# Routing the second expert stage earlier: its first four groups inside the attention's last two turns, its second part beside the first tiles

## The chip, the cores and the metric

One core of a Trainium2 chip runs one program. Its engines work side by side, each through its own instruction list, in order: TensorE (PE, matrix products and transposes into the eight PSUM banks; PEld is its weight load), VectorE (DVE), ScalarE (ACT), GpSimd (POOL) and SyncE (SP, which here only starts DMAs). An engine stops at a wait until a semaphore has reached a value, and all that stands behind the wait in its list stops with it. The metric is the device time of one execution, in microseconds (us).

## The reference, cut to what matters

The program is a stack of six residual blocks on x, which is 4 x 1024 tokens of 128 channels. The change touches the end of the second and the start of the third:

```python
x = x + 0.5 * _L0_ffn_ref(_layernorm(x), router_w, w_gate, w_up, w_down)       # n = 0, experts
x = x + _L0_attn_ref(_layernorm(x), w_qkv, b_qkv, w_proj, b_proj)              # n = 1, attention
x = x + 0.5 * _L0_ffn_ref(_layernorm(x), router_w, w_gate, w_up, w_down)       # n = 2, experts again
x = x + 0.5 * _L1_ffn_ref(_layernorm(x), ...)                                  # n = 3, fp4 products
x = x + _L1_attn_ref(_layernorm(x), ...)                                       # n = 4, retention
x = x + 0.5 * _L1_ffn_ref(_layernorm(x), ...)                                  # n = 5, fp4 products

# the expert block: 8 experts of width 256, each token goes to two of them
logits = x @ router_w.T
weights, selected = sparsemixer_eval(logits, 0.01)     # two largest scores, with masked softmax weights
for e in range(8):
    h = silu(x @ w_gate[e].T) * (x @ w_up[e].T)
    out = out + dense_w[:, e:e + 1] * (h @ w_down[e].T)
```

The attention has 16 heads of 8 channels over 1024 tokens, a softmax, and the product with `w_proj`.

## The kernel before, in words

**Tokens.** The 4096 tokens are 32 tiles of 128; four tiles are a group (8 groups of 512 tokens), and four groups are a part (2 parts of 2048 tokens). x stays on chip.

**An expert stage (n = 0 and n = 2).** For each group: the layer norm (`ln_stats` and `ln_scale` on VectorE, the power -0.5 in `ln_power` on GpSimd, `moe_tokens` writes the normalised tokens, on VectorE), the transposes (`moe_transposes`, TensorE), their copy to SBUF (`moe_copy`, ScalarE), the router's product (`moe_logits`, TensorE) and the copy of the scores (`moe_scores`, VectorE). For each part of four groups: `route` (23 small VectorE instructions: the two best experts of each token), `moe_counts` (2 products on TensorE that count tokens), `find_places` (14 VectorE instructions: in which slot each token lands, ending in `place`, and which expert each tile of slots has, `expert_of`), `moe_exp` (one Exp on ScalarE) and `weigh` (4 VectorE instructions). Then `moe_scatter` writes the part's tokens into the slots in DRAM (`slots_x`): 32 indirect DMAs of 128 tokens, issued by GpSimd one after another. Each expert's slots are filled up to whole tiles of 256, 23 tiles for each part, 46 in all.

The tile loop is written out. At step i TensorE does `turned(i + 2)` (2 transposes, after the tile's slots have been loaded), `gate_up(i + 1)` (8 products, after its weights have been loaded) and `down(i)` (8 products); ScalarE copies, applies Silu and copies the result; VectorE multiplies (`hidden(i + 1)`, L732); SP loads the slots of tile i + 4 and then the weights of tile i + 3 (`moe_sp`). SP waits for all 32 scatters of a part at the first slots load of that part, tile 0 and tile 23. The results go back to DRAM and are gathered by 64 more indirect DMAs and added to x. Beside the loop of stage 2, VectorE does one step of later work (`beside`: the fp4 weights of the next block) in each of i = 0 to 19 and again from i = 35.

**The attention (n = 1).** It has 16 groups of heads and a turn i = 0 to 16 that is written out in 16 steps n; a turn runs the row maxima of group i beside the products of group i - 1. In a step TensorE makes four transposed score tiles (L1082; three banks in a ring, so it waits for ScalarE's Exp, L1171), and 4 products with the values (`values`, L1094, 8 records). Turn 16 has no maxima. Into it, at fixed steps, the kernel before puts the output projection of groups 0 to 5 (`att_project`, L1059), the transposes and the router's products of groups 0 to 3, and on VectorE `att_add` and the layer norms. `route` of the first part stands at the end of turn 16.

**Around the change.** The sums of the last heads leave by SP (8 small DMAs into OC and SC), VectorE inverts them (`att_reciprocals`, two halves of 512 columns, L1210) and GpSimd multiplies them into OC (`normalised`, L1315). The projection of group 7 needs the second half of that. After it come groups 6 and 7 (projection, add, layer norm), then the transposes and scores of groups 4 to 7, then `route`, `moe_counts`, `find_places` and `weigh` of the second part, and only then the first tile. TensorE waits for both parts' places before `turned(0)`. GpSimd's order is: `ln_power` 0 to 5, the two `normalised`, 8 scatters, `ln_power` 6 and 7, 24 scatters, and 32 scatters of part 1.

Of the kernel before, what the change touches and what calls it, by code (L numbers as in the profile page):

```python
# [82 lines left out]
def macaron(nc, a, out):  # L83
    ctx = ExitStack()
    with ctx:
# [253 lines left out]
        COUNTS = {0: 5, 2: 3}  # L339
# [50 lines left out]

        def part_tiles(part):

            return slice(part * PART_TOKEN_TILES, (part + 1) * PART_TOKEN_TILES)
# [6 lines left out]
        def moe_counts(pe, n, part):  # L400
            s = moe
            pe.wait_ge(s["members"], parts_before(n) + part + 1)
            of = members[:, :, :].rearrange("p e t -> p (e t)")
            pe.matmul(bank(COUNTS[n])[:, 2 * P:3 * P], before_in_tile, of, start=True, stop=True)
            pe.matmul(bank(COUNTS[n])[:, 3 * P:4 * P], all_ones, of, start=True, stop=True).then_inc(s["counts"], 1)

        def route(dve, chain, n, part):
# [13 lines left out]
            chain.mark(dve.tensor_reduce(m[0], S, AX.X, ALU.max))  # L421
            chain(dve.tensor_scalar(A.bitcast(I32), S.bitcast(I32), 0x7FFFFFFF, None, ALU.bitwise_and))
            chain.mark(dve.tensor_tensor(F, A, b(m[0]), ALU.max))
            chain.mark(dve.tensor_tensor(X[0], S, b(m[0]), ALU.subtract))
            chain.mark(dve.tensor_tensor(O1, S, b(m[0]), ALU.is_equal))
            chain(dve.tensor_tensor(D, b(m[0]), S, ALU.subtract))
            chain.mark(dve.scalar_tensor_tensor(K[0], F, JITTER, D, ALU.mult, ALU.is_ge))
            chain(dve.tensor_tensor(O1, O1, R, ALU.mult))
            chain(dve.tensor_reduce(tops, O1, AX.X, ALU.max))
            chain(dve.tensor_tensor(O1, R, b(tops), ALU.is_equal))  # L430
            chain(dve.tensor_scalar(M, O1, -1.0, 1.0, ALU.mult, ALU.add))
            chain(dve.tensor_tensor(M, M, S, ALU.mult))
            chain(dve.scalar_tensor_tensor(M, O1, MASKED, M, ALU.mult, ALU.add))
            chain(dve.tensor_reduce(m[1], M, AX.X, ALU.max))
            dve.tensor_tensor(X[1], M, b(m[1]), ALU.subtract).then_inc(s["shifted"], 1)
            chain.mark(dve.tensor_tensor(F, A, b(m[1]), ALU.max))
            chain.mark(dve.tensor_tensor(O2, M, b(m[1]), ALU.is_equal))
            chain(dve.tensor_tensor(D, b(m[1]), S, ALU.subtract))
            chain.mark(dve.scalar_tensor_tensor(K[1], F, JITTER, D, ALU.mult, ALU.is_ge))
            chain(dve.tensor_tensor(O2, O2, R, ALU.mult))  # L440
            chain(dve.tensor_reduce(tops, O2, AX.X, ALU.max))
            chain(dve.tensor_tensor(O2, R, b(tops), ALU.is_equal))
            dve.tensor_tensor(members[:, :, :].rearrange("p e t -> p t e"), O1, O2, ALU.add).then_inc(s["members"], 1)

        def weigh(dve, chain, n, part):
# [4 lines left out]
            chain(dve.tensor_tensor(shifted[:, :, t, :], shifted[:, :, t, :], kept[:, :, t, :], ALU.mult))  # L450
            chain(dve.tensor_reduce(mult[:, :, t], shifted[:, :, t, :], AX.X, ALU.add))
            chain(dve.reciprocal(mult[:, :, t], mult[:, :, t]))
            dve.tensor_scalar(mult[:, :, t], mult[:, :, t], 0.5, None, ALU.mult).then_inc(s["weighed"], 1)

        def find_places(dve, chain, n, part):
# [4 lines left out]
            earlier, in_tile = (bank(COUNTS[n])[:, (2 + k) * P:(3 + k) * P] for k in range(2))  # L460
            until_flat, slot_flat = (v[:, :, :].rearrange("p e t -> p (e t)") for v in (until, slot))
            chain(dve.tensor_tensor_scan(until_flat, restart, in_tile, 0.0, ALU.mult, ALU.add))
            chain.mark(dve.tensor_tensor(slot_flat, until_flat, in_tile, ALU.subtract))
            chain(dve.tensor_scalar(whole_tiles[:, :], until[:, :, PART_TOKEN_TILES - 1], 1.0 / SLOTS_TILE,
                                    (SLOTS_TILE - 1) / (2.0 * SLOTS_TILE), ALU.mult, ALU.add))
            chain.mark(dve.tensor_tensor(slot_flat, slot_flat, earlier, ALU.add))
            chain(dve.tensor_scalar(whole_tiles[:, :], whole_tiles[:, :], ROUND, ROUND, ALU.add, ALU.subtract))
            chain(dve.tensor_tensor_scan(tiles_until[:, :], all_ones[:, 0:EXPERTS], whole_tiles[:, :], 0.0, ALU.mult, ALU.add))
            chain.mark(dve.tensor_tensor(tiles_before[:, :], tiles_until[:, :], whole_tiles[:, :], ALU.subtract))
            chain(dve.tensor_tensor(passed[:, :, :], tile_number.unsqueeze(2).to_broadcast([P, PART_TILES, EXPERTS - 1]),  # L470
                                    tiles_until[:, 0:EXPERTS - 1].unsqueeze(1).to_broadcast([P, PART_TILES, EXPERTS - 1]), ALU.is_ge))
            chain(dve.tensor_reduce(expert_f[:, :], passed[:, :, :], AX.X, ALU.add))
# [93 lines left out]
        def moe_pe(pe, n):  # L566
# [52 lines left out]
            for i in range(STAGE_TILES):  # L619
# [1594 lines left out]
```

## Time and profile before

| | us |
|---|---|
| Median of 3 runs (1643.71 to 1650.12) | 1645.68 |
| The profiled execution: its own time | 1645.15 |
| Its span in the trace | 1643.3 |
| Busy: PE / DVE / ACT / POOL | 1380.4 / 1185.4 / 939.8 / 482.4 |
| Mean granted TensorE clock, as a share of full speed | 0.928 |

The page of the profile cuts the span in 40 slices of 41 us. A digit is the busy share of a slice in tenths; PEclk is the granted clock of TensorE, of which 9 stands for full speed or near it and 5 for half:

```profile
PE   2379995789999999999999988449987788997787
DVE  5412358649999999999999934534358996888995
ACT  0134441248888888888888875024454446664463
POOL 0773533410000001000000011473466745343211
PEclk9999996779999999999999998569997899998898
```

The attention is the long run of nines up to slice 23. Slices 24 to 26 (986 to 1109 us) are the end of the attention and the start of the second expert stage; the tile loop fills slices 27 to 29.

### The profile page before, as it was taken

To read this page: it belongs to the slowest core of one execution; us is meant where nothing else is said; L and a number is where in the kernel's file an instruction comes from. 1 tells how busy PE (TensorE), PEld (TensorE's weight loads), DVE (VectorE), ACT (ScalarE), POOL (GpSimd) and SP (SyncE) were. 2 spreads that over 40 slices of the span, in tenths; PEclk is the share of its full clock that TensorE was granted. 3 is DMA by queue.
4 is the path that set the end of the run, shared out by engine and by line. 5 is a ranking of instruction groups with operands and counts; after the bars stand their busy time and mean duration, and the time that the engine had idled before them with its cause. 6 is when DMAs were issued, how large, how long until landed. Compare 5 with 4: busy or idle time off the path is not lost.

```text
span 1643.3 us, 25865 instructions
## 1 busy us (share of the span) xinstructions
PE 1380.4 (84%) x9137; PEld 716.8 (44%) x9137; DVE 1185.4 (72%) x1894; ACT 939.8 (57%) x1965; POOL 482.4 (29%) x758
## 2 busy tenths in 40 slices
PE   2379995789999999999999988449987788997787
PEld 2279872331111111111111123349975565665576
DVE  5412358649999999999999934534358996888995
ACT  0134441248888888888888875024454446664463
POOL 0773533410000001000000011473466745343211
PEclk9999996779999999999999998569997899998898
DMA  7178753210000010001001000348861000000000
GB/s 246 46 210 241 225 177 102 64 60 20 26 26 25 26 41 25 25 30 35 25 25 41 10 8 4 116 131 261 257 193 31 18 1 1 2 2 2 1 26 26
DMA packets 97455, 116.22 MB, mean 71 GB/s; under 512 B 14368, under 2 KB 76512, under 8 KB 97104
## 3 DMA queue, kind: packets, MB, share of 16 engines
q1 hardware_dynamic: 64112, 85.72, 17.6%
q0 software_dynamic: 8192, 16.79, 3.3%
q10 hardware_dynamic: 25024, 12.06, 2.5%
q8 instruction: 73, 1.20, 0.3%
q14 instruction: 54, 0.44, 0.1%
HBM read 82.28 MB, written 35.26 MB: 72 GB/s over the span
## 4 chain that ended last, share of the span: by engine, by line
PE 57%; DVE 13%; ACT 6%; issue 5%; POOL 3%; SPq 0%; DMA 0%; POOLq 0%; ACTq 0%; DVEq 0%
PE PS L1094 15%; PE PS L1082 11%; PE PS L1071 6%; PE PS L585 5%; DVE neg_half L1225 4%; ACT probs L1171 3%; PE PS L597 3%; PE PS L1681 3%; PE PS L1769 2%; PE PS L1779 2%; POOL came L502 1%; POOL qk_all L1597 1%; PE PS L1712 1%; DVE x L516 1%; PE PS L890 1%
## 5 line engine op out<-in xcount | busy, mean ns | idle before, releaser
L1225 DVE TENSOR_REDUCE neg_half<-PS 128x2 f32<-128x1024 f32 x512 | 601.7, 1220 | 63.0 <-PE PS L1071 47.5
L1171 ACT ACTIVATE probs<-PS 128x512 f32<-128x512 f32 x1024 | 528.9, 604 | 118.5 <-PE PS L1082 118.3
L1082 PE MATMUL PS<-qk_all 51*128 51x512 bf16 x1024 | 279.9, 388 | 17.9 <-ACT probs L1171 12.3
L1094 PE MATMUL PS<-probs,Vg 128*32 128x512 f32 x2048 | 278.6, 617 | 0.0
L1082 PEld LDWEIGHTS PS<-qk_all 51*128 51x128 bf16 x1024 | 71.6, 93 | 338.7 <-ACT probs L1171 319.6
L732 DVE TENSOR_TENSOR shared<-shared,PS 128x512 f32<-128x512 f32 x92 | 63.2, 687 | 208.3 <-PE PS L585 185.6
L1071 PE MATMUL PS<-qk_all 48*128 48x512 bf16 x1024 | 196.3, 396 | 15.7 <-DVE neg_half L1225 13.5
L585 PE MATMUL PS<-slotsT,w_ring 128*128 128x256 f32 x736 | 180.3, 389 | 0.9 <-issue 0.9
L502 POOL DMA_INDIRECT came<-slots_y,place x128 | 128.4, 1003 | 120.0 <-DMA slots_y<-slots_out 83.0
L585 PEld LDWEIGHTS PS<-slotsT,w_ring 128*128 128x128 f32 x736 | 137.0, 196 | 16.8 <-issue 1.1
L487 POOL DMA_INDIRECT slots_x<-tokens_all,place x128 | 125.5, 980 | 41.9 <-issue 38.5
L1301 POOL CAST neg_p<-neg 128x32 bf16<-128x32 f32 x16 | 3.4, 213 | 405.0 <-DVE neg L1232 405.0
L1071 PEld LDWEIGHTS PS<-qk_all 48*128 48x128 bf16 x1024 | 49.5, 95 | 137.7 <-DVE neg_half L1225 131.1
L1681 PE MATMUL PS<-wguT,plane 128*128 128x352 f32 (+4 forms) x384 | 97.0, 415 | 4.1 <-ACT plane L1618 2.5
L597 PEld LDWEIGHTS PS<-w_ring,shared 128*128 128x128 f32 x736 | 96.8, 192 | 6.2 <-DVE shared L732 0.9
L597 PE MATMUL PS<-w_ring,shared 128*128 128x128 f32 x736 | 97.3, 275 | 0.6 <-ACT slots_out L654 0.6
L654 ACT ACTIVATE slots_out<-PS 128x256 f32<-128x256 f32 x92 | 35.3, 383 | 105.9 <-PE PS L597 103.4
L1944 DVE TENSOR_TENSOR shared<-PS,probs 128x512 f32<-128x512 f32 x128 | 79.4, 682 | 17.8 <-PE PS L1769 17.8
L1681 PEld LDWEIGHTS PS<-wguT,plane 128*128 128x128 f32 x384 | 70.3, 216 | 25.4 <-issue 8.5
L1597 POOL TENSOR_TENSOR qk_all<-qk_all 128x704 f32<-128x704 f32 x32 | 43.8, 1390 | 117.6 <-DVE qk_all L1444 93.6
L1690 PE MATMUL PS<-ident,qk_all 128*128 128x128 f32 (+1 forms) x192 | 37.7, 334 | 40.4 <-POOL qk_all L1597 30.2
L574 PE MATMUL PS<-ident,slots_in 128*128 128x128 f32 x184 | 36.7, 283 | 41.3 <-DMA slots_in<-slots_x 23.0
(222 smaller groups left out, 1824.4 us busy)
## 6 DMA issues: line engine op xcount, KB each, us to landing
w_ring<-in_w_experts SPq DMA_DIRECT2D x92, 384.0 KB
slots_in<-slots_x SPq DMA_DIRECT2D x92, 128.0 KB
slots_y<-slots_out ACTq DMA_DIRECT2D x92, 128.0 KB, 3.6
split<-qk_all SPq DMA_DIRECT2D x16, 384.0 KB, 3.3
qk_all<-split SPq DMA_DIRECT2D x64, 96.0 KB
qk_all<-split SPq DMA_DIRECT2D x64, 64.0 KB
slots_x<-tokens_all,place POOLq DMA_INDIRECT x128, 2.2
came<-slots_y,place POOLq DMA_INDIRECT x128
```

What stands on the lines that cost most here:

```text
L487: pool.indirect_dma_start(slots_x[part][:, :], bass.IndirectOffsetOnAxis(place[:, k, t:t + 1], 0), tokens_all[:, t, :], None).then_inc(moe ...
L502: pool.indirect_dma_start(came[:, g % 2, j, k, :], None, slots_y[part][:, :], bass.IndirectOffsetOnAxis(place[:, k, g * GT + j:g * GT + j ...
L585: last = pe.matmul(bank(b)[:, f * SLOTS_TILE:(f + 1) * SLOTS_TILE], w[:, u * FFN + f * P:u * FFN + (f + 1) * P], slotsT[:, k % 2, :], star ...
L597: last = pe.matmul(bank(1)[:, j * P:(j + 1) * P], h[:, k % 2, from_h:from_h + P], w[:, 2 * FFN + f * C:2 * FFN + (f + 1) * C], start=(f == ...
L732: dve.tensor_tensor(h[:, k % 2, :], sg[:, k % 2, :], bank(4 + k % 2), ALU.mult).then_inc(s["h"], 1)
L1071: last = pe.matmul(bank(b + strip), qs[at, slot, 0, pair, t * P:(t + 1) * P], qs[at, slot, 1, pair, half * GW:(half + 1) * GW], start=True ...
L1082: pe.matmul(bank(RING_AT + use % RING), qs[rows, slot, 1, pair, kt * P:(kt + 1) * P], qs[rows, slot, 0, pair, half * GW:(half + 1) * GW], ...
L1094: last = pe.matmul(bank(7)[j * 32:(j + 1) * 32, :], Vg[:, r % 2, kt, j, :], probs[:, n % 2, j, :], start=(kt == 0), stop=(kt == BT - 1))
L1171: act.activation(probs[:, n % 2, STRIPS * strip + pair, :], bank(RING_AT + use % RING), ACT.Exp, scale=ATT_SCALE).then_inc(s["exped"], 1)
L1225: dve.tensor_reduce(neg_half[m % 2][:, i % 2, :, at], bank(use_bank(i, m), 2).rearrange("p (s w) -> p s w", s=STRIPS), AX.X, ALU.max, nega ...
L1681: last = pe.matmul(bank(3 * k, 3)[:, to:to + w], xqT[:, (2 * k + j) * P:(2 * k + j + 1) * P], wguT[:, src:src + w], start=True, stop=True)
L1944: dve.tensor_tensor(pd[:, k % 2, g, :, :].rearrange("p j l -> p (j l)"), bank(g), k_decay[:, g * GW:(g + 1) * GW], ALU.mult).then_inc(s["d ...
```

## The change

**In the attention.** The fixed steps for the projections, transposes and router products are moved. They are counted from the start of turn 16, so -3 is step 13 of turn 15. The first part's `moe_counts` is put into turn 16 too. VectorE does `route` of the first part between the additions of groups 3 and 4 and `find_places` between those of groups 4 and 5. GpSimd puts 20 of the first part's 32 scatters among its last instructions of the attention.

```diff
+        TAIL_PROJECT = {-3: 0, -2: 1, -1: 2, 1: 3, 9: 4, 12: 5}
+        TAIL_TRANSPOSES = {1: 0, 2: 1, 4: 2, 5: 3}
+        TAIL_LOGITS = {2: 0, 4: 1, 5: 2, 7: 3}
+        TAIL_COUNTS = 11
...
-                    if not first:
-                        g = n // 2
-                        if n % 2 == 1 and g < TAIL_GROUPS:
...
-                            att_project(pe, g, g % 2)
-                        if n % 2 == 0 and 4 <= g < 4 + HEAD_GROUPS:
-                            moe_logits(pe, 2, g - 4)
-                        if n % 2 == 0 and 3 <= g < 3 + HEAD_GROUPS:
-                            moe_transposes(pe, 2, g - 3)
+                    tail = STEPS * (i - AG) + n
+                    if tail in TAIL_PROJECT:
...
+                        att_project(pe, g, g % 2)
+                    if tail in TAIL_LOGITS:
+                        moe_logits(pe, 2, TAIL_LOGITS[tail])
+                    if tail in TAIL_TRANSPOSES:
+                        moe_transposes(pe, 2, TAIL_TRANSPOSES[tail])
+                    if tail == TAIL_COUNTS:
+                        moe_counts(pe, 2, 0)
...
+            tail_add(0)
+            tail_add(1)
+            moe_tokens(dve, 2, 0)
+            tail_add(2)
+            moe_tokens(dve, 2, 1)
+            moe_scores(dve, 2, 0)
+            tail_add(3)
+            moe_tokens(dve, 2, 2)
+            moe_scores(dve, 2, 1)
+            moe_tokens(dve, 2, 3)
+            moe_scores(dve, 2, 2)
+            moe_scores(dve, 2, 3)
+            at_once(route(dve, chain, 2, 0))
+            tail_add(4)
+            at_once(find_places(dve, chain, 2, 0))
+            tail_add(5)
             att_reciprocals(dve, BATCH - 1, 0, GW)
+            att_reciprocals(dve, BATCH - 1, GW, SEQ)
...
-            for g in range(HEAD_GROUPS + 2):
+            for g in range(TAIL_GROUPS - 1):
                 ln_power(pool, 2, g)
+            moe_scatter(pool, 2, 0, 0, 2)
+            ln_power(pool, 2, TAIL_GROUPS - 1)
+            moe_scatter(pool, 2, 0, 2, 4)
             normalised(BATCH - 1, BATCH, 0, GW)
+            moe_scatter(pool, 2, 0, 4, 10)
             normalised(BATCH - 1, BATCH + 1, GW, SEQ)
```

**In the expert stage.** `route`, `find_places` and `weigh` become generators, which give up control after each instruction; `at_once` runs one to its end. In stage 2 the second part's three run beside the tiles: six instructions behind each `hidden(i + 1)` from i = 0. Their counting products stand behind `down(4)`, in a bank of their own (7), and their Exp stands in ScalarE's list at i = 4, between two Silus. TensorE's wait for the places is dropped for this stage. The later work beside the loop starts at i = 8 and runs to i = 22.

```diff
+        ROUTE_OPS, COUNTS_TILE, EXP_TILE = 6, 4, 4
...
-            moe_counts(pe, n, 1)
-            pe.wait_ge(s["place"], parts_before(n) + PARTS_MOE)
+            if n == 0:
+                moe_counts(pe, n, 1)
+                pe.wait_ge(s["place"], PARTS_MOE)
+            pe.wait_ge(s["xT"], groups_before(n) + GROUPS)
+            pe.wait_ge(s["logits"], groups_before(n) + GROUPS)
...
                 down(i)
+                if n == 2 and i == COUNTS_TILE:
+                    moe_counts(pe, n, 1)
...
+                if n == 2 and i == EXP_TILE:
+                    moe_exp(act, n, 1)
...
-                moe_scatter(pool, 2, 0, 0, 4)
+                moe_scatter(pool, 2, 0, 10, 14)
                 ln_power(pool, 2, GROUPS - 2)
                 ln_power(pool, 2, GROUPS - 1)
-                moe_scatter(pool, 2, 0, 4)
+                moe_scatter(pool, 2, 0, 14)
             moe_scatter(pool, n, 1)
...
+            second_part = itertools.chain(route(dve, chain, n, 1), find_places(dve, chain, n, 1), weigh(dve, chain, n, 1))
+            if n == 0:
+                at_once(second_part)
             hidden(0)
             for i in range(STAGE_TILES):
                 if i + 1 < STAGE_TILES:
                     hidden(i + 1)
+                for _ in range(ROUTE_OPS):
+                    next(second_part, None)
...
-                if n == 2 and (i < PART_TILES - 3 or at >= BESIDE_AT):
+                if n == 2 and (8 <= i < PART_TILES or at >= BESIDE_AT):
                     next(beside, None)
```

## Rows read from the trace of the kernel before

**Rows 1.** Chain of waits, 905 to 1100 us: start, duration, what

```profile
1029.55 0.61 ACT OTs L1178
...
1036.84 3.35 DVE SC L1210
...
1072.35 19.32 issue
```

**Rows 2.** Timeline of GpSimd: start, duration, instruction, idle time before and its releaser

```profile
1040.27 1.26 POOL L1315 TENSOR_TENSOR shared<-shared,SC 128x512 f32<-128x512 f32 x1 [22.19 <-DVE SC L1210]
1044.96 1.09 POOL L487 DMA_INDIRECT slots_x<-tokens_all,place  x1 [3.42 <-DVE place L480]
...
1054.92 2.03 POOL L325 TENSOR_TENSOR rstd<-aggr,minus_half 128x4 f32<-128x4 f32 x2
...
1086.36 0.95 POOL L487 DMA_INDIRECT slots_x<-tokens_all,place  x1 [0.30 <-issue]
...
1118.42 1.67 POOL L487 DMA_INDIRECT slots_x<-tokens_all,place  x1 [0.30 <-issue]
...
1128.60 0.96 POOL L487 DMA_INDIRECT slots_x<-tokens_all,place  x1 [0.30 <-issue]
```

**Rows 3.** Timeline of SP's queue at the first slots load

```profile
1088.59 3.38 SPq L540 DMA_DIRECT2D slots_in<-slots_x  x5
```

**Rows 4.** Timeline of VectorE: route and find_places of part 0

```profile
1024.29 0.29 DVE L421 TENSOR_REDUCE r_largest<-scores 128x16 f32<-128x128 f32 x1
...
1030.19 0.37 DVE L443 TENSOR_TENSOR p_members<-r_chosen 128x128 f32<-128x128 f32 x1
...
1040.11 0.36 DVE L462 TENSOR_TENSOR_SCAN p_until<-moe_const,PS 128x128 f32<-128x128 f32 x1
...
1044.48 0.18 DVE L480 CAST place<-p_place_f 128x32 uint32<-128x32 f32 x1
```

**Rows 5.** Timeline of TensorE, the attention's last steps

```profile
958.98 1.06 PE L1094 MATMUL PS<-probs,Vg 128*32 128x512 f32 x8
...
961.43 1.06 PE L1094 MATMUL PS<-probs,Vg 128*32 128x512 f32 x8
...
976.49 1.06 PE L1094 MATMUL PS<-probs,Vg 128*32 128x512 f32 x8
...
980.03 1.06 PE L1094 MATMUL PS<-probs,Vg 128*32 128x512 f32 x8
...
993.53 1.07 PE L1094 MATMUL PS<-probs,Vg 128*32 128x512 f32 x8
...
997.51 1.06 PE L1094 MATMUL PS<-probs,Vg 128*32 128x512 f32 x8
...
1016.53 1.94 PE L1094 MATMUL PS<-probs,Vg 128*32 128x512 f32 x8
...
1020.28 1.93 PE L1094 MATMUL PS<-probs,Vg 128*32 128x512 f32 x8
```

**Rows 6.** Windows of 4 us: busy time by engine, granted clock, DMA share, GB/s

```profile
968.00:972.00 4.00, 3.40 (x13) 1.30 (x14) 0.00 (x0) 2.02 (x5) 0.00 (x0) 0.58 0.23 33
```

**Rows 7.** Timeline of TensorE, the first tiles

```profile
1090.91 0.66 PE L574 MATMUL PS<-ident,slots_in 128*128 128x128 f32 x2 [17.05 <-issue]
...
1095.52 0.38 PE L574 MATMUL PS<-ident,slots_in 128*128 128x128 f32 x2
```

**Rows 8.** Timeline of VectorE, the tile loop

```profile
1097.72 0.69 DVE L732 TENSOR_TENSOR shared<-shared,PS 128x512 f32<-128x512 f32 x1 [1.26 <-PE PS L585]
...
1160.16 0.69 DVE L732 TENSOR_TENSOR shared<-shared,PS 128x512 f32<-128x512 f32 x1 [2.15 <-PE PS L585]
```

**Rows 9.** Timeline of ScalarE: Exp, table load and the stage's last result

```profile
1070.40 0.42 ACT L398 ACTIVATE r_shifted<-r_shifted 128x256 f32<-128x256 f32 x1 [6.33 <-DVE r_shifted L435]
1070.84 1.28 ACT L664 ACT_TABLE_LOAD   x1
...
1225.00 0.38 ACT L654 ACTIVATE slots_out<-PS 128x256 f32<-128x256 f32 x1 [1.31 <-PE PS L597]
```

More of the change, by code:

```diff
@@ L7 @@
 from concourse import mybir
+import itertools
 from contextlib import ExitStack
@@ L389, in moe_scores, with at_once @@
                             bank(LOGITS[n][g % 2])[:, 0:GT * EXPERTS].rearrange("p (t e) -> p t e", e=EXPERTS)).then_inc(s["logits"], 1)
+        def at_once(steps):
+            for _ in steps:
+                pass
         def part_tiles(part):
@@ L403, in moe_counts @@
             of = members[:, :, :].rearrange("p e t -> p (e t)")
-            pe.matmul(bank(COUNTS[n])[:, 2 * P:3 * P], before_in_tile, of, start=True, stop=True)
-            pe.matmul(bank(COUNTS[n])[:, 3 * P:4 * P], all_ones, of, start=True, stop=True).then_inc(s["counts"], 1)
+            pe.matmul(bank(COUNTS[n][part])[:, 2 * P:3 * P], before_in_tile, of, start=True, stop=True)
+            pe.matmul(bank(COUNTS[n][part])[:, 3 * P:4 * P], all_ones, of, start=True, stop=True).then_inc(s["counts"], 1)
         def route(dve, chain, n, part):
@@ L748, in moe_dve @@
                 dve.wait_ge(ld["small"], 48)
-            route(dve, chain, n, 0)
-            if n == 2:
-                att_reciprocals(dve, BATCH - 1, GW, SEQ)
-            find_places(dve, chain, n, 0)
-            weigh(dve, chain, n, 0)
+            if n == 0:
+                at_once(route(dve, chain, 0, 0))
+                at_once(find_places(dve, chain, 0, 0))
+            at_once(weigh(dve, chain, n, 0))
             if n == 2:
@@ L771, in moe_dve @@
             moe_scores(dve, n, GROUPS - 1)
-            route(dve, chain, n, 1)
-            find_places(dve, chain, n, 1)
-            weigh(dve, chain, n, 1)
+            second_part = itertools.chain(route(dve, chain, n, 1), find_places(dve, chain, n, 1), weigh(dve, chain, n, 1))
+            if n == 0:
+                at_once(second_part)
             hidden(0)
@@ L1188, in turn @@
                         exps(i - 1, n, 1)
-                    if i == AG and n % 2 == 1 and 3 <= n // 2 < 3 + HEAD_GROUPS:
-                        g = n // 2 - 3
+                    tail = STEPS * (i - AG) + n
+                    if tail in TAIL_TRANSPOSES:
+                        g = TAIL_TRANSPOSES[tail]
                         if g == 0:
@@ L1261, in att_dve, with tail_add @@
             dve.wait_ge(s["biased"], GROUPS)
-            for g in range(TAIL_GROUPS):
+            def tail_add(g):
                 att_add(dve, g, g % 2)
```

63 lines of the change are left out of this document (50 added, 13 removed).

## The prediction, on record before the changed kernel ran

> **What bounds the kernel now.** I read three views, in this order. The chain of waits comes first, around the end of the attention [rows 1]. The attention's last values end at 1029.5, the sums travel through SP, VectorE inverts them from 1036.8, and further on there are 19.3 us of "issue" from 1072.35: nothing that the profile names holds the chain, so it is a wait on something whose records lie on another engine. The timeline of GpSimd says what [rows 2]. Its first scatter starts at 1044.96, right behind `place` of part 0, which VectorE ends at 1044.66 [rows 4]; the last of the 32 starts at 1086.36 and ends at 1087.3. SP starts the slots load at 1088.59 [rows 3], 1.27 us later, and TensorE's first tile starts at 1090.91 [rows 7], 2.32 us after that. So the first tile is bound neither by TensorE nor by the second part's routing, but by one sum:
>
> first tile = place of part 0 + 46.25 us.
>
> In it are 32 scatters in 42.35 us less two `ln_power` (2.2 with the gaps), so 40.15 us or 1.26 each, 0.3 before and 3.6 behind. The third view is the tile loop on VectorE: a `hidden` takes 0.69 and waits 2.15 for TensorE [rows 8], so TensorE sets 2.84 us a tile and VectorE has 2.15 us free in each. From the first tile to the stage's last result, at 1225.0 [rows 9], it is 134.1 us.
>
> **Where place of part 0 comes to lie.** A bare attention step takes 2.45 us (958.98 to 961.43), one with a projection 3.54 (976.49 to 980.03), so a projection costs 1.09; one with a router product and transposes 3.98 (993.53 to 997.51), so the pair costs 1.53, of which some 0.5 for the transposes [rows 5]. Inserted work costs its full length, before and after alike, for TensorE waits for an Exp in each step and ScalarE for TensorE in turn. Steps 13, 14 and 15 of turn 15 take 3 x 3.54 from 958.98: step 0 of turn 16 starts its values at 969.6. Steps 0 to 6 are three bare ones (7.35), step 1 with projection and transposes (4.1) and three with a pair (11.9), and I add 1.0 because ScalarE now copies each transposed group right before the next step's Exps: step 7 at 994.0. The last router product ends at 996.1, the copy of the scores takes 0.2, `route` takes 6.3 (1024.29 to 1030.56) [rows 4]: members at 1002.5. The counts stand in step 11, after 3.4 + 2.45 + 3.54 + 2.45, so at 1005.9, and end at 1007.4; VectorE waits for them, not they for VectorE. `find_places` takes 4.55 (1040.11 to 1044.66): place at 1012.0 at full clock.
>
> The granted clock fell to 0.58 in 968 to 972 [rows 6], in steps like these, after bare steps; a half-clock step (1.2 GHz) takes 3.75 (1016.53 to 1020.28) instead of 2.45. I take two such steps before the counts, 2.6 us: place at 1014.6. Bounds: 1012.0, and 1035 if all from step 0 on runs at half clock (11 steps x 1.3, and 9 us of inserted work that would double). I take the low side, because the clock came back from 972 on in the same kind of steps; the ends stay in the range.
>
> **The first tile.** GpSimd now has more between the 32 scatters: `ln_power` of group 5 (1.0 and a gap) and both `normalised` (1.26 each and gaps [rows 2]), 4.2 us in all. First tile = 1014.6 + 46.25 + 4.2 = 1065.05, which is 25.9 earlier. What could be late next:
> - The second `normalised` stands behind 20 scatters and is reached at 1042.9. Its input needs the attention's end (I get 1022 to 1026), 7.3 us of SP and landing (1029.55 to 1036.84 [rows 1]) and 3.35 of `att_reciprocals`: 1033 to 1037. So GpSimd is late, not the sums, and 6 us or more of a slow attention end cost nothing.
> - TensorE's way to `turned(0)`. `ln_power` 6 and 7 stand behind 8 more scatters, at 1055.5 for group 6. Tokens (1.1), then two groups at 3.5 each with the low clock of an idle TensorE, and the last copy: 1064. That is within 1.3 us of the scatters. If it loses, the price is one to two us.
> - SP's weights for tiles 0 to 2 and the later weights go out before the scatters end; nothing is queued behind them that is due.
>
> **The loop.** It gains two count products behind `down(4)`, 0.5 us on the engine that sets the pace. VectorE's six instructions a tile are 1.2 to 2.3 us and lie in the free 2.15; `hidden` is due only one tile later. The 24th instruction waits for the counts, and `hidden(5)` stands behind it; TensorE needs its result only after the next `gate_up`, 1.7 us later, so it is covered. ScalarE's Exp at i = 4 stands between Silus. The trace has Exp, then a table load of 1.28 us, then Silu, with 0.02 us between [rows 9]: two switches and the Exp are 3.0 us, where `down(5)` has some 3 us of room behind the previous result. I take 0.2. The loop then costs 0.7 more, from 0.5 to 3.
>
> The Trainium skill (ScalarE: Activation LUTs, What ACT_TABLE_LOAD costs) states about 1.38 us of drain beside the 1.28 us load, 2.66 us for each switch. The row shows the load and no drain beside it. By the page ScalarE would be held for 5.7 us, and the loop would lose about 2.7 us more.
>
> **The second part's first tile, the wait that comes in place of the old one.** Before, part 1's scatters started at once behind part 0's and ended at 1129.6, long before tile 23. Now they wait for `place` of part 1, the 37th instruction beside the tiles, so behind `hidden(7)`. `hidden(1)` starts 6.8 us after the first tile (1097.72 against 1090.91 [rows 7, 8]), six tiles more are 17.0, its own length and the instruction 0.8, the loop's new cost 0.7: 25.3 after the first tile. The 32 scatters took 41.9 us here (1087.6 to 1129.56, a few of them stretched like that at 1118.42 [rows 2]): they end at +67.5, SP at +68.8, TensorE at +71.1. `turned(23)` is due 21 tiles after `turned(2)` (4.6 after the first tile [rows 7]), at +64.9 with the new cost. TensorE stops for 6.2 us. SP's list has the slots of tile 23 ahead of the weights of tile 22, so these are held back too, and `gate_up(22)` is next on TensorE: between 0 and 2.84 (a tile's loads keep up with one tile), I take 1.2. Sum 7.4 us; with scatters at their bare 40.1 us and no late weights it is 4.4, with a clock that falls in the gap some 10. TensorE sets the pace, so it catches nothing up.
>
> **The rest.** The steps beside the loop were 20 + 11 and are 15 + 11, with 25 of them holding work: the last now comes at i = 44 rather than 39, still before ScalarE gets to its product behind the loop. The gathers move with the tiles. Nothing from 1225 on changes its order.
>
> **The sum.** 25.9 - 0.7 - 7.4 = 17.8 us less. The profiled execution took 1645.15 (span 1643.3), so 1627.35; the median shown is 0.5 higher: **1627.9 us**.
>
> **The rivals.**
> - *A, no stop at tile 23* (8%): part 1's scatters would have to be some 7 us quicker than they were. Against it: each of the 128 needs its 1.26 us of GpSimd. Time 1620.5.
> - *B, the clock eats the attention's end* (9%): half of the steps from step 0 on run at half clock, place comes at 1023.6, 9 us later than I say, and with it every scatter and the first tile: 1636.9. For it: the dip at 968 [rows 6]. Against: the inserted work keeps TensorE busier there than the bare steps did.
> - *C, slower than before: the scatters stretch* (4%). All of part 1's scatters and 20 of part 0's now run while VectorE works in short instructions. The one at 1118.42 took 1.67 instead of 0.96 [rows 2], beside a 0.95 us instruction. If each of part 1's took 1.97 with its gap instead of their mean of 1.31, the stop at tile 23 would grow by 21 us: 1649. It decides from 1.87 us for each, where the gain is gone. Against it: most of part 1's scatters of before lay beside the fp4 steps and the sum grew by only 1.8 us. The Trainium skill (SBUF — State Buffer, Who interferes with whom) states the mechanism: VectorE's two-port copies and tensor_scalars lock GpSimd out of the port on which it writes descriptors, and the loser waits to the end of the instruction. The row shows a stretch of 0.7 us at most.
> - *D, TensorE's way to the first tile is much later, or the list does not run as I read it* (3%): 1645.
>
> The forecast holds with 76%, its own range 1622 to 1635. For 8 in 10 I go to 1621 and 1637, which takes in B and the bounds of the stop and of the table switches, but not place at 1035. A measurement of this kernel tells about 0.5%, 8.2 us, from no change. Faster by more than that (below 1637.5): the forecast, A and a part of B, 88%; within it 7%; slower 5%.
>
> **What would show it.** In the changed kernel: `place` of part 0 at 1012 to 1017, behind it 20 scatters before the attention's sums are normalised; the first tile 50.4 us behind place; a table load on each side of the Exp at the fifth tile with TensorE's pace nearly kept; one gap of 6 to 9 us on TensorE at tile 23, released by the slots load, and the next wait at the weights; 142 us from the first tile to the last result. The forecast is wrong if place comes after 1022, if the gap at tile 23 is missing or above 12 us, or if the loop's pace of 2.84 us breaks in the first eight tiles.

## The result, and the profile after

The changed kernel takes 1632.99 us (median of 5 runs, 1632.65 to 1635.42) beside 1647.02 for the one before on the same chip (5 runs, 1643.71 to 1652.0): ratio 0.9914, 95% interval 0.9892 to 0.9936, so 14.0 us less. The forecast was 1627.9, 17.8 us less. The profiled execution takes 1632.65, span 1630.8: 12.5 us less than the profiled one of before. One thing about all times here: the same instructions at the attention's end take longer in some executions (place of part 0 comes 64.2 to 64.3 us behind the last `neg` in three traces of such code, 75.0 in two, where TensorE's clock stayed at its lower level for longer), so a number from a profile is compared with one from a like execution, or counted from that `neg`. That `neg` is a VectorE instruction of the last row maxima and stands ahead of the change; here before, then after:

```profile
953.03 0.19 DVE L1232 TENSOR_TENSOR neg<-neg_half 128x32 f32<-128x32 f32 x1
```

```profile
951.83 0.19 DVE L1296 TENSOR_TENSOR neg<-neg_half 128x32 f32<-128x32 f32 x1
```

**Place of part 0.** TensorE's steps 7 to 11 of turn 16 (start, length, engine, line, operation, idle before):

```profile
992.15 1.06 PE L1155 MATMUL PS<-probs,Vg 128*32 128x512 f32 x8
...
995.81 1.93 PE L1155 MATMUL PS<-probs,Vg 128*32 128x512 f32 x8
...
999.56 1.93 PE L1155 MATMUL PS<-probs,Vg 128*32 128x512 f32 x8
1001.43 2.08 PE L1120 MATMUL PS<-wproj,shared 128*128 128x128 f32 x8
...
1005.32 1.93 PE L1155 MATMUL PS<-probs,Vg 128*32 128x512 f32 x8
...
1009.08 1.93 PE L1155 MATMUL PS<-probs,Vg 128*32 128x512 f32 x8
1010.94 0.80 PE L410 MATMUL PS<-p_members,moe_const 128*128 128x128 f32 x2
```

Step 7 is at 992.15, or 993.35 counted as before (forecast 994.0). From step 8 to step 11 the values take 1.93 instead of 1.06, and a bare step takes 3.75 instead of 2.45. Windows of the same stretch give the length, each engine's busy time (PE, PEld, DVE, ACT, POOL), then the granted clock (0.71 and 0.50 here), the DMA share and GB/s:

```profile
994.00:996.00 2.00, 1.47 (x10) 0.52 (x13) 1.66 (x8) 1.38 (x3) 0.00 (x0) 0.71 0.00 0
996.00:1012.00 16.00, 15.03 (x56) 3.99 (x49) 6.47 (x27) 7.45 (x15) 1.01 (x1) 0.50 0.05 9
```

The reader sees a granted clock of 0.50 (1.2 GHz) for 16 us: four steps and not two. VectorE, which waited 6.38 us for the counts, and GpSimd, which starts behind it:

```profile
1012.13 0.42 DVE L495 TENSOR_TENSOR_SCAN p_until<-moe_const,PS 128x128 f32<-128x128 f32 x1 [6.38 <-PE PS L411]
...
1015.89 0.18 DVE L526 CAST place<-p_place_f 128x32 uint32<-128x32 f32 x1
```

```profile
1016.36 1.09 POOL L534 DMA_INDIRECT slots_x<-tokens_all,place  x1 [9.52 <-DVE place L526]
...
1043.72 1.28 POOL L1391 TENSOR_TENSOR shared<-shared,SC 128x512 f32<-128x512 f32 x1
...
1061.16 0.96 POOL L534 DMA_INDIRECT slots_x<-tokens_all,place  x1 [0.30 <-issue]
```

Place ends at 1016.07, where [rows 4] had 1044.66. The second `normalised`, at 1043.72, finds its input long there (VectorE's second reciprocal ended at 1034.92). The last scatter of part 0 starts at 1061.16 ([rows 2]: 1086.36), SP loads the slots at 1063.39 ([rows 3]: 1088.59), and TensorE starts at 1065.72 ([rows 7]: 1090.91), 49.65 behind place:

```profile
1063.16 1.87 PE L383 MATMUL PS<-wr,plane 128*128 128x8 f32 x8 [0.69 <-ACT plane L374]
1065.72 0.66 PE L621 MATMUL PS<-ident,slots_in 128*128 128x128 f32 x2 [0.69 <-DMA slots_in<-slots_x]
```

TensorE's own work (the last router product, to 1065.03) ends only 0.69 before it.

**The loop.** ScalarE around its Exp shows a load on each side, and nothing between instructions (the copy ahead of the first load ends at 1082.83):

```profile
1082.85 1.28 ACT L404 ACT_TABLE_LOAD   x1
1084.15 0.42 ACT L404 ACTIVATE r_shifted<-r_shifted 128x256 f32<-128x256 f32 x1
1084.58 1.28 ACT L701 ACT_TABLE_LOAD   x1
...
1085.87 0.60 ACT L701 ACTIVATE shared<-PS 128x512 f32<-128x512 f32 x1
```

Place of part 1 ends at 1091.86, 26.1 behind the first tile (forecast 25.3). TensorE at tiles 22 to 24, and SP at that time:

```profile
1128.03 0.38 PE L621 MATMUL PS<-ident,slots_in 128*128 128x128 f32 x2
...
1136.36 0.69 PE L621 MATMUL PS<-ident,slots_in 128*128 128x128 f32 x2 [5.33 <-DMA slots_in<-slots_x]
1138.60 3.44 PE L632 MATMUL PS<-slotsT,w_ring 128*128 128x256 f32 x8 [1.55 <-issue]
...
1142.78 0.38 PE L621 MATMUL PS<-ident,slots_in 128*128 128x128 f32 x2
```

```profile
1134.33 0.36 SPq L587 DMA_DIRECT2D slots_in<-slots_x  x1
1135.46 0.36 SPq L578 DMA_DIRECT2D w_ring<-in_w_experts  x1
```

The last scatter ends at 1133.06; the slots load behind it releases `turned(23)` at 1136.36, due at 1130.87; the weights, issued 1.13 behind the slots, hold `gate_up(22)` for another 1.55 (the row names no releaser; experiment 3 shows that it is the weights), and it then takes 3.44 instead of the 1.89 of full clock. `turned(24)` is 9.07 late. The stage's last result is at 1210.17 ([rows 9]: 1225.00), 14.8 earlier, and everything behind runs shifted by 14.78 until TensorE's last products: they run at half clock for longer in this execution than in that of before, and with the last store 2.3 us are lost there. That loss is not the change's: from the stage's last result to the end of the span the eleven traces of this case take 418.3 to 423.0 us, with the same instructions.

### The profile page after: what moved, and what is told of

Its sections match the earlier page's. It is cut to its first block, busy times and chain, and to the rows that moved or that the text cites. A ratio compares the mean times of both kernels' runs of the same rounds, so it can differ in the third digit from the quotient of the medians.

```text
span 1630.8 us, 25871 instructions
## 1 busy us (share of the span) xinstructions
PE 1382.1 (85%) x9134; PEld 718.4 (44%) x9137; DVE 1184.8 (73%) x1894; ACT 942.1 (58%) x1967; POOL 482.8 (30%) x758
## 4 chain that ended last, share of the span: by engine, by line
PE 54%; DVE 12%; POOL 7%; ACT 6%; issue 5%; DMA 0%; POOLq 0%; ACTq 0%; DVEq 0%
PE PS L1155 15%; PE PS L1143 11%; PE PS L1132 6%; DVE neg_half L1289 4%; POOL slots_x L534 4%; ACT probs L1234 3%; PE PS L632 3%; PE PS L1761 3%; PE PS L1849 2%; PE PS L644 2%; PE PS L1859 2%; POOL came L549 1%; PE PS L1792 1%; DVE x L563 1%; POOL qk_all L1677 1%
## 5 line engine op out<-in xcount | busy, mean ns | idle before, releaser
L1143 PE MATMUL PS<-qk_all 51*128 51x512 bf16 x1024 | 280.4, 389 | 17.8 <-ACT probs L1234 12.3
L2024 DVE TENSOR_TENSOR shared<-PS,probs 128x512 f32<-128x512 f32 x128 | 79.4, 682 | 17.8 <-PE PS L1849 17.8
L701 ACT ACTIVATE shared<-PS 128x512 f32<-128x512 f32 x92 | 54.9, 597 | 25.6 <-PE PS L632 24.8
```

What stands on the lines that cost most here:

```text
L1143: pe.matmul(bank(RING_AT + use % RING), qs[rows, slot, 1, pair, kt * P:(kt + 1) * P], qs[rows, slot, 0, pair, half * GW:(half + 1) * GW], ...
L2024: dve.tensor_tensor(pd[:, k % 2, g, :, :].rearrange("p j l -> p (j l)"), bank(g), k_decay[:, g * GW:(g + 1) * GW], ALU.mult).then_inc(s["d ...
```

## The experiments

All are edits of the changed kernel. The first four ran together (before: 1647.78, 14 runs), the next three together (before: 1649.96, 11 runs), the last two together (before: 1649.12, 11 runs).

**1. The scatters back behind the attention.**

```
-            moe_scatter(pool, 2, 0, 0, 2)
             ln_power(pool, 2, TAIL_GROUPS - 1)
-            moe_scatter(pool, 2, 0, 2, 4)
             normalised(BATCH - 1, BATCH, 0, GW)
-            moe_scatter(pool, 2, 0, 4, 10)
             normalised(BATCH - 1, BATCH + 1, GW, SEQ)
...
-                moe_scatter(pool, 2, 0, 10, 14)
+                moe_scatter(pool, 2, 0, 0, 4)
                 ln_power(pool, 2, GROUPS - 2)
                 ln_power(pool, 2, GROUPS - 1)
-                moe_scatter(pool, 2, 0, 14)
+                moe_scatter(pool, 2, 0, 4)
```

> The changed kernel with one part undone: GpSimd's 20 scatters inside the attention go back behind both normalised, as in the kernel before; the rest of the change stays. Theory (GpSimd's 32 scatters of part 0 set the first tile, so the gain is how early they begin): they now begin at about 1036.4, behind the second normalised; with 40.1 us of scatters, 2.2 us of ln_power and 3.6 us of landing and load the first tile comes at about 1082.4, 16.7 us later than in the changed kernel (1065.7); own time about 1649. Rival 1 (the earlier routing and the quicker end of the attention carry the gain): within 3 us of the changed kernel, 1633 to 1636. Rival 2 (the dropped wait of TensorE for the places carries it): the same, within 3 us.

Measured: 1649.74 (10 runs, 1648.19 to 1661.83), ratio 1.0035, interval 1.0011 to 1.0059; profiled 1648.49. Place of part 0 is still at 1016.45, and GpSimd starts its scatters only behind `normalised`:

```profile
1035.30 1.31 POOL L1391 TENSOR_TENSOR shared<-shared,SC 128x512 f32<-128x512 f32 x1 [12.12 <-DVE SC L1274]
1036.79 1.09 POOL L534 DMA_INDIRECT slots_x<-tokens_all,place  x1 [0.17 <-issue]
```

The first tile is at 1082.66, 16.9 later than in the changed kernel: that much of the 25.2 are the 20 scatters that run while the attention ends. The other 8.2 stay (it was at 1090.91 before), because `place` and `normalised` come earlier. They don't show in the time because this kernel keeps the stop at tile 23: from the first tile to the last result it takes 144.84 us, where the kernel before took 134.1. So the early routing without the early scatters gains 8.2 us at the first tile and loses 10.7 in the loop.

**2. The second part routed ahead of the first tiles.**

```
-            if n == 0:
-                moe_counts(pe, n, 1)
+            moe_counts(pe, n, 1)
+            if n == 0:
                 pe.wait_ge(s["place"], PARTS_MOE)
...
-            if n == 0:
-                at_once(second_part)
+            at_once(second_part)
```

(and the Exp ahead of the first Silu; the calls inside the loop go)

> The changed kernel with the other part undone: the second part is routed ahead of the first tile again (route, counts, find_places, weigh and the Exp), but TensorE does not wait for its places. Theory (the stop at tile 23 comes from the late place of part 1): first tile about 7.4 us later, at 1073.1 (6.3 of route and 1.4 of counts behind the last scores), find_places hidden before the first hidden; no stop at tile 23 (9.1 us less) and 0.9 us less in the first tiles; own time about 1630.5, 2 us less than the changed kernel. Rival (the stop is one of DMA traffic or of the ring of slots, not of the place): the stop stays, and the time is about 1640.

Measured: 1629.26 (5 runs, 1627.86 to 1640.29), ratio 0.9893, interval 0.9877 to 0.9910. The profiled execution is the long one. Tiles 22 and 23 in it:

```profile
1142.76 0.38 PE L621 MATMUL PS<-ident,slots_in 128*128 128x128 f32 x2
...
1145.60 0.38 PE L621 MATMUL PS<-ident,slots_in 128*128 128x128 f32 x2
```

Place of part 1 stands 4.2 behind the first tile instead of 26.1, the stop is gone, and the loop takes 133.93 instead of 144.45. Of the 10.5 us, 7.0 are paid ahead of the first tile (it is 56.6 behind place of part 0, not 49.65: counts and routing stand in its way); the rest, 3.5, is what the times show (3.7). The interleaving in the change cost more by its stop than it hid.

**3. The weights of tile 22 ahead of the slots of tile 23.**

```
+                weights_first = n == 2 and i + IN_RING == PART_TILES
+                if weights_first:
+                    moe_load_weights(sp, n, i + W_RING - 1)
                 if i + IN_RING < STAGE_TILES:
                     moe_load_slots(sp, n, i + IN_RING)
```

> The changed kernel, and SP issues the weights of tile 22 ahead of the slots of tile 23 (one swap in its list). Theory (the weights were held back in SP's list behind the wait for the scatters): TensorE's first gap of 5.3 us at tile 23 stays, the second of 1.5 us behind it goes; own time 1.5 to 2.5 us less, about 1631. Rival (the second gap is DMA latency or the low clock): no change, 1632.6 within 0.5 us.

Measured: 1632.57 (5 runs, 1629.79 to 1641.71), ratio 0.9917, interval 0.9888 to 0.9946. Two of the five are long ones; the other three have 1629.79, 1629.87 and 1632.57. By the trace, which is of a long one:

```profile
1147.70 0.69 PE L624 MATMUL PS<-ident,slots_in 128*128 128x128 f32 x2 [5.58 <-DMA slots_in<-slots_x]
1148.19 3.10 PE L635 MATMUL PS<-slotsT,w_ring 128*128 128x256 f32 x8
...
1152.02 0.38 PE L624 MATMUL PS<-ident,slots_in 128*128 128x128 f32 x2
```

The first gap stays, the second is gone: `turned(24)` is 4.32 behind `turned(23)`, not 6.42. So 2.1 us of the stop were the order of two lines. The times alone would not have told it: their interval overlaps that of the changed kernel, as those of experiments 2, 5 and 7 do.

**4. More of the second part's routing ahead of the tiles.**

```
-        ROUTE_OPS, COUNTS_TILE, EXP_TILE = 6, 4, 4
+        ROUTE_AHEAD, ROUTE_OPS, COUNTS_TILE, EXP_TILE = 18, 7, 1, 2
...
+            for _ in range(ROUTE_AHEAD):
+                next(second_part, None)
```

> The changed kernel with the second part's routing begun earlier: 18 of its 41 VectorE instructions stand ahead of the first hidden, where VectorE is idle for 5.4 us, then 7 a tile instead of 6; counts behind down(1), Exp at i = 2. Theory: place of part 1 comes at about 1080.5 instead of 1091.9, its scatters end at about 1121.7, before the slots of tile 23 are due; the stop of 9.1 us goes and nothing replaces it; own time about 1623.6. Rival (VectorE's instructions then delay hidden, which sets TensorE's pace): the first four tiles lose 3 us or more, own time above 1626. Rival (the stop is DMA traffic): it stays, 1632.

Measured: 1622.77 (4 runs, 1622.16 to 1623.07), ratio 0.9851, interval 0.9835 to 0.9868; 1623.6 were expected; first tile at 1066.36, place of part 1 at 1084.04 (3.5 later than expected, its counts stood behind `down(1)` and `hidden(3)` behind the table loads), the loop 136.21. `turned(23)` and what is behind it:

```profile
1132.01 0.38 PE L621 MATMUL PS<-ident,slots_in 128*128 128x128 f32 x2
1132.83 1.97 PE L632 MATMUL PS<-slotsT,w_ring 128*128 128x256 f32 x8 [0.44 <-issue]
...
1135.52 0.38 PE L621 MATMUL PS<-ident,slots_in 128*128 128x128 f32 x2
```

`turned(24)` is 0.67 late instead of 9.07, and the loop 8.2 us shorter. With 2 this shows that the stop came from the late place of the second part, and most of it needn't be paid for ahead of the tiles: the first tile comes as early as in the changed kernel (113.8 behind the last `neg`, there 113.9).

**5. The counts in step 9 instead of 11.**

```
-        TAIL_COUNTS = 11
+        TAIL_COUNTS = 9
...
+                    if tail == TAIL_COUNTS:
+                        moe_counts(pe, 2, 0)
                     if tail in TAIL_PROJECT:
...
-            tail_add(4)
             at_once(find_places(dve, chain, 2, 0))
+            tail_add(4)
```

> One edit to the changed kernel: the two count products of part 0 come in step 9, ahead of the projection of group 4, instead of step 11, and find_places comes ahead of the addition of group 4. My theory: in the changed kernel place of part 0 was late because the counts stood in step 11, behind steps at half clock, and everything up to the first tile is a chain from place: first tile = place + 49.65. The counts' input (members) was ready about 1001, so they come at about 1001.4 instead of 1010.9 and place some 9 us earlier, about 1006.6. The second normalised is then reached on GpSimd at about 1034.3, just when its input (1034.9) is ready. First tile about 1056.5 to 1057, own time about 1623.5. Rival: the attention's sums, or TensorE's way through the last two groups' logits (0.7 us of slack in the changed kernel), become the bound; then place still comes 9 us earlier and the first tile gains less than 6 us, own time 1627 or more.

Measured: 1631.08 (6 runs, 1624.98 to 1635.19), ratio 0.9887, interval 0.9857 to 0.9918. Three executions lie at 1634.78 to 1635.19 with a mean clock of 0.927, three at 1624.98 to 1627.39 with 0.934 to 0.936; the changed kernel's five began at 1632.65. The median misses the 1623.5 expected, and the profiled execution is a long one. It has to be compared with the long ones of 2 and 3, which have the counts in step 11: there place comes 75.0 behind the last `neg`, here 65.55, so it is 9.4 earlier, as expected. But the first tile is 118.7 behind the last `neg`, and 124.8 in 3: 6.2 earlier, not 9. GpSimd tells why:

```profile
1017.39 1.01 POOL L326 TENSOR_TENSOR rstd<-aggr,minus_half 128x4 f32<-128x4 f32 x1 [37.36 <-DVE aggr L321]
1018.58 1.09 POOL L534 DMA_INDIRECT slots_x<-tokens_all,place  x1 [0.18 <-issue]
```

Place was there at 1015.20, but `ln_power` of group 4 stands ahead of the scatters in GpSimd's list, and its input had moved behind `find_places` by this very edit. The first scatter starts 3.4 us behind place instead of 0.3: my own omission.

**6. The three edits together** (3, 4 and 5).

> The three edits that helped by my theory, together: 18 instructions of the second part's routing ahead of hidden(0) and 7 a tile after it, with its counts at tile 1 and its Exp at tile 2; the first part's counts in step 9 (as in e5_counts_early); the weights of tile 22 issued ahead of the slots of tile 23. If they are independent terms: the run with the routing ahead stood at 1622.8, less what e5_counts_early gains on the changed kernel (8 to 9), less the 0.7 of the late gate_up: about 1613.5. Rival: with the first tile earlier the early routing instructions do not find their inputs sooner (the last groups' logits, which come from the attention's sums), so members of part 1 and the stop at tile 23 keep their absolute time and 3 us or more come back as a stop: 1617 or more.

Measured: 1620.58 (6 runs, 1617.12 to 1630.43), ratio 0.9848, interval 0.9817 to 0.9879. The profiled one, 1617.12, is a short one: place of part 0 at 1006.46 (54.8 behind the last `neg`; 64.2 in the changed kernel), the same 3.4 us to the first scatter, first tile 1059.54, no stop at tile 23 (`turned(22)` to `turned(24)` in steps of 2.84), loop 136.78. 1613.5 expected plus the 3.1 by which the first scatter is later is 1616.6, so in this execution the terms add up. The median does not reach it (7.1 above the 1613.5): two of the six took 1626.74 and 1630.43, with a mean clock of 0.927 and 0.924. The rival (the second part's routing keeps its absolute time) came in small part: counted from the last `neg`, place of part 1 is 4.7 earlier than in 4 and the first tile 6.0, and the loop is 0.6 longer, but no stop comes back.

**7. Needless products in three bare steps.**

```
+                    if tail in (6, 8, 10):
+                        for j in range(GT):
+                            pe.matmul(bank(0 if tail == 6 else 2)[:, 0:P], OC[:, j * P:(j + 1) * P], wproj[:, :], start=True, stop=True)
```

> The changed kernel with four needless 128x128 products (those of a projection, their result unused) in each of the steps 6, 8 and 10 of turn 16, which were bare. In the changed kernel the granted clock fell to 0.50 from about 995 to 1012, over steps 8 to 11. Theory 1, the clock falls because TensorE idles between the products of bare steps: with the fill it stays at 1.00, steps 8 to 11 cost 2.45 each instead of 3.75, 5.2 to 6.4 us less with the inserted work, the fill costs 3 x 1.09 = 3.3, place of part 0 at 1012.5 to 1014, some 2 to 3 us earlier, own time about 1630.5. Theory 2, the clock falls whatever TensorE does here (a limit on the work of the steps before): the fill runs at half clock for the most part, 5 to 6 us are added, place at about 1022 and own time about 1638; the attention's end also comes later.

Measured: 1629.59 (6 runs, 1628.49 to 1639.23), ratio 0.9895, interval 0.9866 to 0.9925. The windows, the changed kernel first, then this one:

```profile
988.00:998.00 10.00, 8.29 (x48) 2.31 (x47) 3.45 (x15) 6.88 (x14) 0.00 (x0) 0.84 0.00 0
998.00:1008.00 10.00, 9.35 (x35) 2.63 (x32) 4.68 (x20) 4.62 (x10) 1.01 (x1) 0.50 0.08 14
```

```profile
988.00:998.00 10.00, 8.56 (x63) 4.08 (x55) 0.89 (x5) 5.67 (x12) 0.00 (x0) 1.00 0.00 0
998.00:1008.00 10.00, 8.67 (x60) 3.99 (x60) 7.43 (x31) 6.41 (x13) 1.01 (x1) 1.00 0.08 16
```

The clock stays at 1.00, each filled step takes 3.54, and place comes 61.2 behind the last `neg` instead of 64.2: more work, done earlier. The 64.2 is not one chance execution: the traces of 1 and 4 have 64.25 and 64.29, with the same steps. Five of the six executions have a mean clock of 0.935 or 0.936, all five of the changed kernel 0.930 or 0.931. So theory 1's forecast came, with 3.1 us (2 to 3 forecast), and theory 2's did not. What exactly lets the clock fall is not shown by it: in the changed kernel it fell at 995, behind the bare step 6 and step 7 with a router product, in each of which TensorE waited 0.53 for an Exp, but it waited as long in the bare step 3 (from 979.17) and the clock stayed at 1.00. One execution of six is long all the same (1639.23, mean clock 0.928).

**8. GpSimd's order mended**, on top of 6.

```
-            for g in range(TAIL_GROUPS - 1):
+            for g in range(TAIL_GROUPS - 2):
                 ln_power(pool, 2, g)
             moe_scatter(pool, 2, 0, 0, 2)
-            ln_power(pool, 2, TAIL_GROUPS - 1)
+            ln_power(pool, 2, TAIL_GROUPS - 2)
             moe_scatter(pool, 2, 0, 2, 4)
+            ln_power(pool, 2, TAIL_GROUPS - 1)
             normalised(BATCH - 1, BATCH, 0, GW)
-            moe_scatter(pool, 2, 0, 4, 10)
+            moe_scatter(pool, 2, 0, 4, 9)
```

(the later calls begin at 9 and 12 instead of 10 and 14)

> e6_all_three with GpSimd's order mended: ln_power of group 4 comes behind the first four scatters (in e6_all_three it stood ahead of all of them and waited for the addition of group 4, which had moved behind find_places, so the first scatter came 3.39 us behind place instead of 0.3), that of group 5 behind eight, and the second normalised behind 18 scatters instead of 20, because in e6_all_three TensorE's way (second normalised to last router product, 21.3 us) ended only 0.6 before the first tile. My theory: scatters start at place + 0.35 again, the last one ends 47.8 behind place, first tile = place + 51.3 instead of + 53.1, so 1.8 us earlier; own time about 1615.3 in an execution with a clock like e6's profiled one (1617.1). Rival: the sums of the last half (second reciprocal ended 1032.5) or TensorE's way are already the bound, and it gains less than 0.7 us.

Measured: 1624.28 (5 runs, 1618.95 to 1625.55), ratio 0.9828, interval 0.9809 to 0.9846. The profiled execution, 1625.55, had the long stretch of low clock: place of part 0 at 1017.19, 65.5 behind the last `neg` as in the long one of 5, where 6 had 54.8. From place on it is as expected: first scatter 0.3 behind it, first tile 50.7 behind it (51.3 expected; 53.1 in 6). The order is worth 2.4 us from place on; that the five times don't show it in the median fits their clocks (1625.55, 1624.41 and 1624.28 with 0.928 to 0.930, 1618.95 and 1619.7 with 0.934 and 0.933).

**9. The same with four needless products in each of steps 6 and 8.**

> e8_pool_order with four needless products in the steps 6 and 8 of turn 16. If the clock rises with them as in e7_filled_steps (1.00 up to 1018, where the changed kernel had 0.50 from 995 to 1012): the two steps cost 2.2 us, and steps 8 and 9 with the counts lose 2.5 to 3.5 us less, so place of part 0 comes 0.5 to 1.5 us earlier than in e8_pool_order in like executions, and fewer executions are some 10 us longer (2 of 6 were in e6_all_three, 1 of 6 in e7_filled_steps). Median 1614 to 1615. Rival: what is gained at full clock is paid for the fill, place comes at the same time or up to 2 us later, and the share of long executions stays the same.

Measured: 1618.60 (6 runs, 1615.04 to 1630.21), ratio 0.9821, interval 0.9795 to 0.9846; before took 1649.12 beside it. Profiled (1615.04), the clock at 1.00 up to 1018; the last window of that stretch:

```profile
1008.00:1018.00 10.00, 7.87 (x52) 2.55 (x54) 5.59 (x13) 7.38 (x15) 8.22 (x9) 1.00 0.12 47
```

Place comes 54.7 behind the last `neg`, in 6 it was 54.8 without the fill: with the counts already in step 9 the fill pays only for itself, so the rival came and the 1614 to 1615 expected for the median was missed. One of six executions is long; in 8 the profiled one was. Whether the fill makes long ones rarer is not settled by so few. Its interval overlaps those of 6 and 8; with it the lowest time and the lowest median of the series stand at 1615.04 and 1618.60, below both kernels of the case.

## Why the prediction was right, and where it was short

The mechanism was right in its main steps: first tile = place plus a fixed sum, 20 scatters before the sums are normalised, a stop at tile 23 of two parts, and nothing behind the stage. Experiment 1 ties 16.9 of the 25.2 us at the first tile to the scatters, 2 and 4 tie the stop to the second part's place. Some luck was in it: all five runs of the changed kernel were of the short kind. The prediction put a clock that stays low for half of the steps into its rival B, with 9%; in experiments 2 and 3 three of ten executions were long, and such a one lies some 10 us higher, outside the forecast's own range. The sizes, in the profiled executions:

- **Place of part 0** was 2.7 us later than forecast, counted from the last `neg` (1.2 us were gained ahead of it, outside the change). The step of the prediction that failed is "I take two such steps": four steps, with their inserted projection and the counts, ran at half clock. From step 7 to the start of `find_places` it took 19.98 us, where the prediction's full-clock sum has 13.4, so 6.6 us went there instead of 2.6. I chose two because the clock had come back in like steps at 972. With the bare steps 6, 8 and 10 filled (experiment 7) the clock stayed up. `find_places` took 3.94 instead of 4.55, and step 7 came 0.65 early, once the 1.2 us are taken out; both made the error smaller. The 0.6 of `find_places` is one instruction: before, its third one began while GpSimd ran `normalised` (1040.27 to 1041.53 in [rows 2]) and ended just behind it, after 0.85 instead of the 0.17 that it takes in the changed kernel:

```profile
1040.71 0.85 DVE L464 TENSOR_SCALAR p_whole<-p_until 128x8 f32<-128x8 f32 x1
```

- **From place to the first tile**: 49.65 against 50.45, 0.8 in its favour. That TensorE's way comes within 1.3 us was right (0.69).
- **The loop's small costs**: 0.86 by tile 8 against 0.7 forecast, of them 0.44 the counts, the rest ScalarE. Of the Trainium skill's rule (ScalarE: Activation LUTs, What ACT_TABLE_LOAD costs), 2.66 us a switch with its drain, the trace shows 1.28 for each of the two loads and 0.02 beside them; the 2.7 us more that the prediction estimated from the page did not come.
- **The stop at tile 23**: 9.07 against 7.4. Its first part was 5.5 against 6.2, the weights' part 3.6 against 1.2: the sum left out the clock that falls in the gap, so that `gate_up(22)` took 3.44 instead of 1.89; the prediction had named it as the case of "some 10", and that is the one that came. Experiment 3 takes 2.1 us of it away.
- **Behind the loop's middle**: some 0.4, a `down` that waits 0.17 for VectorE's steps beside the loop, not forecast.

So 17.8 - 2.7 + 0.8 - 2.3 = 13.6 for the stage; plus 1.2 ahead of it and less 2.3 of clock and store at the very end it is the 12.5 of the profiled executions. Rival A (no stop) was excluded by the trace. Rival B, the clock, is the one that came in part: some 4 of its 9 us in the profiled execution, and more than all of it in others of the experiments (in 2 the clock was 0.50 to 0.52 from 988 to 1028, and place stood 75.0 behind the last `neg`, 13.4 more than forecast). Rival C did not come: of part 1's 32 scatters two stretched, to 1.47 and 1.25 us, and all took 40.92, less than the 41.9 of before. The stretches are 0.8 us in all. The first of them, and VectorE at that time:

```profile
1108.25 0.95 DVE L1448 TENSOR_TENSOR qk_all<-qk_all 128x768 f32<-128x768 f32 x1
```

```profile
1108.56 1.47 POOL L534 DMA_INDIRECT slots_x<-tokens_all,place  x1 [0.30 <-issue]
```

The Trainium skill (SBUF — State Buffer, Who interferes with whom) names two-port copies and tensor_scalars as what locks GpSimd out of the port on which it writes descriptors; of a tensor_tensor with both inputs in SBUF it says that it contends with GpSimd's reads. In the trace both stretched scatters began inside such a tensor_tensor (L1448, and L1466 at 1122.44), so that these transfers are held up beside it too. Each was stretched by what was left of that instruction less 0.13 us: 0.64 left and 0.51 more here, 0.42 and 0.29 at 1122.97, and in the kernel before 0.84 and 0.71 at 1118.42. A scatter already under way was not stretched (1119.17, with L1456 from 1119.60, took 0.96). Nor were the two that began inside the reciprocal of 1018.10 to 1021.45, which reads one input: 0.96 each. So in these traces it mattered where a scatter started and beside what, and none lost more than 0.71 us.

## What to carry to other kernels

Where GpSimd issues a long row of indirect transfers (1.26 us each here), what counts is when the first can go and what stands in its list; start them in the shadow of the stage before, and after moving any instruction look again at each list that it feeds. Work put in small pieces beside a loop has its own due time: 37 instructions at six a tile let the 32 scatters behind them end 5.5 us too late, which cost 9.07 us with the weights and the clock, and with 18 of them ahead of the loop it was 8.2 us shorter. Where TensorE waits in each of a row of short steps, as at the attention's end here, reckon such a stretch at both clocks and put both into the range: the same steps took 64.2 us in some traces and 75.0 in others. Compare an edit with an execution of the same kind.

## What was not expected of the hardware

Needless products made a stretch shorter: with 12 products more in three steps the granted clock was 1.00 where it had been 0.50 for 16 us, and the steps' end came 3.1 us earlier. And the same instructions get a different clock from one execution to the next, and it falls at a different moment: for good at 979 in experiment 2, at 995 in the changed kernel. Three windows of 20 us had 1.00, 0.67 and 0.90 in the changed kernel, and in experiment 2, which has the same instructions up to here:

```profile
968.00:988.00 20.00, 17.59 (x85) 7.30 (x84) 4.83 (x22) 10.36 (x21) 1.51 (x2) 0.70 0.10 14
988.00:1008.00 20.00, 18.46 (x69) 6.01 (x69) 4.99 (x22) 9.85 (x20) 0.00 (x0) 0.50 0.00 0
1008.00:1028.00 20.00, 18.50 (x69) 6.16 (x68) 8.17 (x33) 8.14 (x17) 3.18 (x4) 0.52 0.05 11
```

The difference is 10.7 us at place of part 0. In the ten traces of the changed kernel and its edits there are two kinds and little between: with the counts in step 11 place comes 64.2 to 64.3 behind the last `neg` or 75.0, with the counts in step 9 54.7 to 54.8 or 65.5 (with the fill of 7 it was 61.2). The four long traces (2, 3, 5 and 8) have a clock of 0.83 in 968 to 978 and 0.54 to 0.65 in 978 to 988, the short ones 1.00 in both. It can stay down for long: in experiment 3 TensorE was busy for 9.1 to 9.4 of every 10 us from 988 to 1018, and the clock stayed at 0.50. What starts the earlier fall stays open.
